# A second attention whose output is made one iteration earlier, with its norms on the scalar engine

## What is computed

```python
x = x + attention_a(layernorm(x))      # 16 heads of 8, rotary positions, causal, then a projection
x = x + experts(layernorm(x))
x = x + attention_b(layernorm(x))
x = x + experts(layernorm(x))          # the same expert weights

def attention_b(h):                    # one head of 128
    q, k, v = h @ WQ, h @ WK, h @ WV
    score = (q @ k.T / sqrt(128)) * band    # outside of the band (32 back, 31 ahead) the score is 0, not masked
    return softmax(score) @ v

def experts(h):                        # 64 experts of 128x128 and 128x128, the best 4 of each row
    s = sigmoid(h @ expert_sel.T)
    gates = s at its four largest, else 0
    return sum over experts e of (relu(h @ keys[e]) * gates[:, e]) @ values[e]
```

## Time and profile before

| | |
|---|---|
| time, median of 3 runs | 1121.22 us (1119.34 to 1125.25) |
| time of the profiled execution | 1114.41 us |
| its span, first to last instruction | 1112.7 us |
| PE busy, mean granted clock | 800.1 us (72%), 0.854 |
| DVE busy | 741.7 us (67%) |
| POOL busy | 727.1 us (65%) |
| ACT busy | 566.7 us (51%) |
| 16 DMA engines | 147 GB/s on average |

### The profile page before, as it was taken

How to read it: one execution, slowest core, us unless ns; L and a number is a source line. 1 busy time by engine, 2 the same in 40 slices (tenths; PEclk the granted TensorE clock), 3 DMA queues, 4 the chain that set the end, 5 groups by cost and what they waited for, 6 DMA issues and landing times.

```text
span 1112.7 us, 22610 instructions
## 1 busy us (share of the span) xinstructions
PE 800.1 (72%) x7290; PEld 584.2 (53%) x7290; DVE 741.7 (67%) x2033; ACT 566.7 (51%) x1513; POOL 727.1 (65%) x860
## 2 busy tenths in 40 slices
PE   1789988788878877679779766655556899898000
PEld 0444443444434432579779765444445888898000
DVE  3687898888878842576465666888979575576111
ACT  1167767675757665456536444444344556465000
POOL 6245748887875758665666462477777656666776
PEclk8689999998989988889979888776667999899555
DMA  6456645543237223359868651011113778898322
GB/s 192 135 197 209 211 164 197 175 137 100 84 94 236 61 70 101 107 161 270 237 172 245 174 141 37 29 50 52 50 52 103 216 215 240 233 270 250 93 61 64
DMA packets 206547, 163.82 MB, mean 147 GB/s; under 512 B 15968, under 2 KB 191072, under 8 KB 206432
## 3 DMA queue, kind: packets, MB, share of 16 engines
q1 hardware_dynamic: 183968, 110.43, 34.4%
q0 software_dynamic: 16384, 33.59, 10.2%
q10 hardware_dynamic: 6080, 18.35, 4.4%
HBM read 78.94 MB, written 83.36 MB: 146 GB/s over the span
## 4 chain that ended last, share of the span: by engine, by line
PE 36%; POOL 19%; DVE 17%; issue 12%; DMA 9%; ACT 6%; POOLq 0%; ACTq 0%; SPq 0%; DVEq 0%
PE ps L789 7%; PE ps L798 6%; POOL sorted_rows L1736 5%; PE ps L690 5%; DMA x_scaled<-result_rows,dest 3%; PE ps L778 3%; PE ps L649 3%; POOL y_heads L1750 2%; ACT arena L1001 2%; POOL arena L1782 2%; DVE row_max L1236 2%; POOL x_scaled L1750 2%; POOL xn L1757 2%; PE ps L698 1%; DVE block_max L1236 1%
## 5 line engine op out<-in xcount | busy, mean ns | idle before, releaser
L1001 ACT ACTIVATE arena<-ps 128x512 f32<-128x512 f32 x320 | 183.0, 598 | 74.5 <-PE ps L622 73.2
L1736 POOL DMA_INDIRECT sorted_rows<-v_aug,dest x128 | 128.4, 1003 | 86.6 <-DVE dest L1423 36.1
L1736 POOL DMA_INDIRECT sorted_rows<-x_scaled,dest x128 | 126.4, 987 | 43.1 <-issue 28.0
L789 PE MATMUL ps<-arena 128*128 128x128 f32 x1024 | 144.9, 287 | 10.3 <-DVE arena L1435 8.9
L1435 DVE COPY arena<-ps 128x512 f32<-128x512 f32 x128 | 88.3, 690 | 94.2 <-PE ps L778 93.7
L649 PE MATMUL ps<-arena 64*128 64x128 bf16 (+3 forms) x576 | 129.0, 302 | 28.5 <-DMA arena<-k_parts 15.1
L1236 DVE TENSOR_REDUCE row_max<-ps 128x1 f32<-128x512 f32 (+1 forms) x192 | 126.9, 681 | 30.7 <-PE ps L669 29.5
L990 ACT COPY arena<-ps 128x512 f32<-128x512 f32 x128 | 74.9, 585 | 137.1 <-PE ps L798 136.9
L798 PE MATMUL ps<-arena 128*128 x1024 | 139.4, 281 | 0.9 <-ACT arena L990 0.9
L789 PEld LDWEIGHTS ps<-arena 128*128 128x128 f32 x1024 | 132.7, 202 | 13.3 <-DVE arena L1435 9.9
L622 PE MATMUL ps<-arena 64*128 64x512 bf16 (+3 forms) x512 | 124.4, 311 | 16.2 <-ACT arena L1001 13.5
(11 more groups left out here) (221 smaller groups left out, 1648.8 us busy)
## 6 DMA issues: line engine op xcount, KB each, us to landing
arena<-sorted_rows SPq DMA_DIRECT2D x128, 256.0 KB
result_rows<-arena SPq DMA_DIRECT2D x128, 256.0 KB
sorted_rows<-arena ACTq DMA_DIRECT2D x16, 1024.0 KB, 5.0
arena<-q_parts SPq DMA_DIRECT2D x16, 512.0 KB, 4.0
arena<-k_parts SPq DMA_DIRECT2D x16, 512.0 KB, 5.0
q_parts<-parts SPq DMA_DIRECT2D x52, 128.0 KB, 2.9
k_parts<-parts SPq DMA_DIRECT2D x38, 128.0 KB, 3.0
sorted_rows<-x_scaled,dest POOLq DMA_INDIRECT x128
```

Source lines behind the costliest of these rows:

```text
L789: mm = pe.matmul(ps[:, e_bank(2, layer, half, n), P * i:P * i + P], ktile[:, v, P * i:P * i + P], xtt[:, v, P * i:P * i + P], start=True, ...
L1001: nc.scalar.activation(prob[:, grp % 2, pr % 2, PROB_AT[u]:PROB_AT[u] + T], ps[:, v % 2, :], ACT.Exp, scale=SCALE_A).then_inc(exp_done, 1)
L1736: g.indirect_dma_start(sorted_d[b // HALF][:, :], bass.IndirectOffsetOnAxis(dest[:, 16 * b + n:16 * b + n + 1], 0), scaled_rows(layer, b)[ ...
```

## The change

1. O of batch b+1 is made in iteration b, no longer O of b. For that PE's list now begins with S01, S23, then RK and VO, and P01, P23, O follow ahead of NT. The banks are dealt out anew.
2. The norms N3 and N2 leave DVE. DVE makes one more small product (minus mean times inverse root), and ACT applies them as `Identity` with a scale and a bias for each row, behind place 6 and ahead of its copy of NT.
3. On ACT the 16 scaled copies now both stand ahead of E, with the copy of VO ahead of them, and E stands directly ahead of the copy of P01.
4. The outside sums move on DVE from behind the norms to behind place 0; the first part of the positions moves from behind place 5 to ahead of it.
5. The rounding in `positions` is one operation, and the running sum starts from the page ends of the batch before, which saves another; the outside sums are one reduction over overlapping windows of five strips, which saves two. Positions are also computed in the first attention, so two operations go there as well.
6. The steps beside: (0, 1) had 16, 14 and 4 in iterations -2, -1 and 0, and now has 14, 11, 5 and, in iteration 1, 4. (1, 0) had 8 and 14 in iterations 7 and 8 and now has 9 and 14.

```diff
-BJOBS = [(7, "P01", 0), (1, "P23", 0), (5, "O", 0), (1, "S01", 1), (3, "S23", 1), (1, "RK", -1), (5, "NT", 0), (6, "LG", 0),
-         (3, "XT", 2), (6, "Q", 2), (7, "K", 2), (3, "V", 2), (5, "VO", 1), (6, "TB", -1)]
+BJOBS = [(1, "S01", 1), (3, "S23", 1), (6, "RK", -1), (7, "VO", 1), (7, "P01", 1), (1, "P23", 1), (5, "O", 1), (3, "NT", 0),
+         (1, "LG", 0), (7, "XT", 2), (3, "Q", 2), (7, "K", 2), (1, "V", 2), (6, "TB", -1)]
-BESIDE = {(0, 1): {-2: (3,) + 13 * (1,), -1: PLACES * (1,), 0: (1, 0, 0, 1, 0, 0, 1, 0, 0, 1, 0, 0, 0, 0)},
-          (1, 0): {7: 6 * (0,) + 8 * (1,), 8: PLACES * (1,)}}
+BESIDE = {(0, 1): {-2: (2,) + 12 * (1,) + (0,), -1: (0, 1, 1, 0) + 9 * (1,) + (0,), 0: (0, 1, 0, 1, 0, 1, 0, 1, 0, 1, 0, 0, 0, 0),
+                   1: (0, 1, 0, 1, 0, 1, 0, 1, 0, 0, 0, 0, 0, 0)},
+          (1, 0): {7: 5 * (0,) + 9 * (1,), 8: PLACES * (1,)}}
...
             for it in range(FIRST_IT_B, LAST_IT_B + 1):
+                attend(it, "S01", "S23")
+                beside(it, 0)
+                attend(it, "RK", "VO")
+                beside(it, 1)
+                beside(it, 2)
                 attend(it, "P01")
-                beside(it, 0)
+                beside(it, 3)
                 attend(it, "P23")
-                beside(it, 1)
+                beside(it, 4)
                 attend(it, "O")
-                beside(it, 2)
-                attend(it, "S01", "S23")
-                beside(it, 3)
-                attend(it, "RK")
-                beside(it, 4)
                 beside(it, 5)
+                beside(it, 6)
                 attend(it, "NT")
-                beside(it, 6)
+                beside(it, 7)
                 attend(it, "LG")
...
+            def apply_norm(i, b, dst, done):
+
+                for t in range(TT):
+                    nc.scalar.activation(dst[:, t, :], x[:, TT * b + t, :], ACT.Identity, bias=negb[:, i, t:t + 1],
+                                         scale=rsb[:, i, t:t + 1]).then_inc(done, 1)
...
+                if name == "N3":
+                    act.wait_ge(shifts, b + 3)
+                    act.wait_ge(scaled, 16 * (B + b - 1))
+                    apply_norm(1, b, xn1[:, b % 2], norm3)
+                    return
+                if name == "N2":
+                    act.wait_ge(shifts, b + 1)
+                    apply_norm(0, b, xn0, norm2)
+                    return
...
                 if 0 <= r < B:
                     act.wait_ge(top_seq, 12 * (B + r) + 12)
                     act.wait_ge(norm3, TT * r + TT)
                     scale(1, r, range(0, 8))
-                beside(it, 2)
-                beside(it, 3)
-                attend(it, "E")
+                beside(it, 1)
                 if 0 <= r < B:
                     scale(1, r, range(8, 16))
-                beside(it, 4)
-                beside(it, 5)
-                attend(it, "NT")
-                beside(it, 6)
+                beside(it, 2)
+                attend(it, "E", "P01")
+                beside(it, 3)
+                attend(it, "P23")
+                for place in (4, 5, 6):
+                    beside(it, place)
+                attend(it, "N3", "N2", "NT")
+                beside(it, 7)
...
+                nc.vector.scalar_tensor_tensor(out=negb[:, lo:hi, :], in0=mvb[:, lo:hi, :, 0], scalar=-1.0, in1=rs,
+                                               op0=ALU.mult, op1=ALU.mult).then_inc(shifts, 1)
...
-                nc.vector.tensor_scalar(near_pages[:, :], part_pages[:, :], MAGIC, None, ALU.add).then_inc(pos_seq, 1)
+                nc.vector.tensor_scalar(pages[:, q, :], part_pages[:, :], MAGIC, -MAGIC, ALU.add, ALU.add).then_inc(pos_seq, 1)
...
-                nc.vector.tensor_tensor_scan(upto[:, :], ones_f[:, :], fresh[:, :], 0.0, ALU.mult, ALU.add).then_inc(pos_seq, 1)
...
-                nc.vector.tensor_scalar(ends[:, h, :], upto[:, :], taken, None, ALU.add).then_inc(pos_seq, 1)
+                nc.vector.tensor_tensor_scan(ends[:, h, :], ones_f[:, :], fresh[:, :], taken, ALU.mult, ALU.add).then_inc(pos_seq, 1)
...
-                nc.vector.tensor_tensor(pairs[:, :], strips[:, 0:15], strips[:, 1:16], ALU.add).then_inc(strip_seq, 1)
-                dve.wait_ge(strip_seq, q + 3)
-                nc.vector.tensor_tensor(four[:, :], pairs[:, 4:11:2], pairs[:, 6:13:2], ALU.add).then_inc(strip_seq, 1)
-                dve.wait_ge(strip_seq, q + 4)
...
-                nc.vector.tensor_tensor(outside[:, :], four[:, :], strips[:, 3:10:2], ALU.add).then_inc(strip_seq, 1)
+                tail = strips[:, 3:14]
+                windows = bass.AP(tail.tensor, tail.offset, [tail.ap[0], (2, TT), (1, 5)])
+                nc.vector.tensor_reduce(outside[:, :], windows, AX.X, ALU.add).then_inc(strip_seq, 1)
...
                 beside(b, 0)
+                if 0 <= b + 1 < B:
+                    outside_sums(b + 1)
                 beside(b, 1)
...
-                if attend:
-                    dve.wait_ge(scaled, 16 * (B + b - 1))
-                    apply_norm(1, b, xn1[:, b % 2], norm3)
-                if prepare:
-                    if far:
-                        bank, n = bjob["XT", far - 1]
-                        dve.wait_ge(bank_ready[bank], n + 1)
-                    apply_norm(0, far, xn0, norm2)
                 beside(b, 4)
-                if 0 <= b + 1 < B:
-                    outside_sums(b + 1)
-                beside(b, 5)
                 if route:
                     bank, n = bjob["RK", r]
                     place_rows = positions(B + r, ps[:, bank, :], bank_ready[bank], n + 1, bank_free[bank], n + 1)
                     advance(place_rows, 6)
+                beside(b, 5)
                 beside(b, 6)
```

58 lines of the change are left out of this document (21 added, 37 removed).

## The result

| | before | after |
|---|---|---|
| time, median of 20 runs each | 1118.28 us (1112.73 to 1127.92) | 1124.33 us (1120.40 to 1130.33) |
| ratio, 95% interval | | 1.005 (1.0032 to 1.0068) |
| profiled execution, its span | 1114.41, 1112.7 us | 1123.67, 1121.9 us |
| PE busy, granted clock | 800.1 us, 0.854 | 812.7 us, 0.855 |
| DVE busy | 741.7 us | 718.8 us |

The changed kernel is 0.5% slower, 5.6 us by the ratio (0.005 of 1118.28; the two medians themselves differ by 6.05). DVE has 23 us less to do, as meant, and the end comes later all the same. The two profiled executions lie 9.3 us apart, more than the runs do. Of that, 2.0 us are there before the changed part begins: the first expert step of half (0, 1) (DVE's copy) is at 559.62 instead of 557.65.

What follows compares the result with a forecast made beforehand. No engine fills the span; POOL's run sets the end, by when destinations of batches 0 and 7 and expert results come. +1.4 and -0.9 gave +0.5 us: 1114.9 profiled, 1121.5 with the 6.8 carried over; range 1110 to 1129.

Steps and rivals of the forecast that it cites:

- rival B: ACT's order: in iteration 5 E, P and N3 wait behind scaled copies whose end POOL decides; slower, 1128 us; 20%.
- first scatter: Start of POOL's run, when batch 0's destinations are ready: 700.6 us, so -5.5, bounds -10 and +1.
- the hold: In iteration 5 ACT's scaled copies of batch 4 wait for POOL's scatter of batch 2, last issued at 810.36 us.
- the ninth step: Iteration 7 has 9 expert steps instead of 8 on the way to batch 7's destinations: +2.2 us.
- Scaled copies of batch 4: Their end on ACT in iteration 5, moved with the first scatter: 812.9 - 5.5 = 807.4 us.
- From there to the choice of batch 5: From the last scaled copy through E, P, O (1.95), NT and LG: 10 us, where it was 4.9.
- The ring: The late round of PE and ACT: 27.7 us at half clock, 24 with some products at full clock, 25.7 taken.
- Choice of batch 6 to the first step of (1, 0): It was 11.9 us; 1.1 of norms less and 0.2 more, so the first step comes at 854.1.
- destinations 7: The moment batch 7's destinations are ready for POOL's scatter: -0.3 + 2.2 - 0.5 = +1.4 us.
- Norm on ACT: Priced like the scaled copy, 0.30 us each, N3 1.2 us on the path to NT; wrong if over 0.4.
- Waits: O's wait gone, PE idle ahead of P01 not NT, S01 waiting 1.1 us for V's copies, scatter 7 about 10.
- Rival A: The early output wins through with PE at full clock, the end following POOL alone: -8.5 to -11.5, about 1111; 27%.

Runs made afterwards that it cites:

- before_swap: The kernel before with other buffers for the scaled rows of batches 4, 5 and 7, so batch 4's copies aren't held by batch 2's scatter; ratio 0.9921.
- Norms_on_dve: The changed kernel with the norms N3 and N2 back on DVE, all else kept; ratio 1.0046.
- before_short: The kernel before with only the shorter positions and outside sums (four DVE operations fewer a batch); ratio 0.9979.
- swap_late_table: swap_homes, and in addition DVE takes the page table of half 0 behind the choice of the next iteration; ratio 0.9911.
- swap_homes: The changed kernel with other buffers for the scaled rows of batches 4, 5 and 7, so ACT doesn't wait for batch 2's scatter; ratio 0.998.
- best1: swap_late_table, and in addition the scaled copies of batches 1 to 5 stand behind V's copies on ACT; ratio 0.991.
- before_swap_short: The kernel before with the buffer exchange of before_swap and the shorter positions and outside sums of before_short; ratio 0.9956.
- best1_old: best1 with the tables of expert steps of the kernel before; ratio 0.9948.

## Why the prediction was right in its number and wrong in its mechanism

I forecast 1121.5 us, and it was 1124.33, inside 1110 to 1129. But that stood on a base of 1121.22 for the kernel before, whose runs beside the changed one have a median of 1118.28. As a difference I said +0.3 us (my sum reads +0.5, and carried over with its 6.8 it gives 1121.7, not 1121.5) and it is +5.6, at the border of what I called no change. What happened is rival B, which I gave 20%: E, P and N3 behind held copies, in the place and nearly at the price that I named (1128 is 6.8 above the base). That the number held is in part luck: B was in the range, not in the forecast. The size is a near match too, since B assumed no gain at the first scatter, where there were 3.1 us, and a cheaper O. And B holds for this pair of kernels: before_swap shows that the hold costs the kernel before as much, and without it the change still stands behind by as much (0.998 against 0.9921), until the page table is taken later. So it is shown where the loss arises in this kernel, and that it goes with the hold; how it divides between the longer chain behind the hold, the longer round and the ninth step is read from single traces alone.

Along the steps, with moments on the clock of the prediction, so 2.0 us of later start taken off:

- *First scatter, 700.6 said.* 704.91 - 1.97 = 702.9. The gain is 3.1 us, not 5.5, inside the bounds of -10 and +1. Norms_on_dve (149.5) shows that it comes from the norms, and before_short that the shorter operations bring none of it (148.6).
- *Scaled copies of batch 4, 807.4 said.* 813.53 - 1.97 = 811.6. Besides the 2.3 from above, POOL's run to there took 1.7 us longer than before. I had taken its pace as fixed, though the rows of its timeline aren't all alike (1.0 and 1.1 us here, and up to 1.9 in places), and the 144 transfers up to scatter 7 take 1.38 us each (199.4 / 144), not the 1.25 to 1.3 that I read.
- *From there to the choice of batch 5, 10.0 said.* It is 11.6 (825.10 - 813.53). **The term that was mis-sized is O: 1.95 said, 3.54 measured.** I took it from the kernel before, where PE goes from Q, K, V through VO and P to O with no idle over 0.91 us. The new order leaves only S, RK, VO and an idle of 6.5 us ahead of P01; I had that idle in the sum and yet kept O at the full clock. Every late round has it.
- *The ring, 24 to 27.7, 25.7 taken.* Measured 28.4 in the last round (853.47 - 825.10), 0.7 above the far end, which had O at 1.9 and not 3.54; the other terms came to 0.9 less. "Nearer the middle" was the choice that failed: the idle of "some 7 us" that I named as the ground for the half clock was there, so the half-clock end was the value to take, for O too.
- *Choice of batch 6 to the first step of (1, 0), 11.0 said:* 11.05. Right.
- *From there to destinations 7, 52.8 said (51.1 + 2.2 - 0.5).* 50.3 (914.83 - 864.52). The ninth step was priced at 2.2 and costs 3.3 in the traces; something else in this stretch is 3.6 us shorter, and I haven't taken it apart. Before_short shows 0.8 of it: 61.7 us from choice 6 to scatter 7 against 63.0, where the sum had 0.5.
- *Norm on ACT, 0.30 us each said.* A single one is 481 ns, and eight take 3.19 us, a pitch of 0.39. The prediction called itself wrong above 0.4 and didn't say of which: the duration is above it, the pitch just below. It costs nothing at the end, since O at the half clock covers it.
- *Waits.* O's wait is gone, PE idles ahead of P01 and not of NT, V's copies hold S01 for 1.15 us: as said. The wait ahead of scatter 7 is 15.42, not about 10. The wait for the page table (9.55 us at 794.39) I hadn't foreseen. TB is last in PE's list, and DVE takes it last in its own iteration; with DVE ahead of PE, it waits there for PE's whole ring. The hold covers it in this kernel; without the hold swap_late_table is 7.7 us below swap_homes by the ratios (0.998 - 0.9911) and 5.0 at the end of the trace.
- *Rival A* (the early output wins through) is what best1 shows for the ring: 22.9 us once the copies are out of E's way. Its price, though, was bounded by POOL, as I said of A ("the end then follows POOL alone").

The largest error of the reasoning is that the 4.9 and 10 us behind the hold were both in my walk, one in each kernel, and I let an early first scatter pay for it. The first scatter was worth 3.1 us, and POOL's run took more than half of it back before it reached the hold.

## What to carry to other kernels

Before work is moved behind a waiting instruction, follow that engine's list and ask which of the instructions ahead is held by another engine's run: the chain behind the hold counts in full, however much idle the engine has elsewhere. When the matrix engine gets only short groups of products between idles, price them by rows at the half clock, all of them. The idle directly ahead doesn't tell it alone: O is at the full clock behind 5.93 us of idle with an expert step in between, and at the half one in best1 behind 2.25 us. And when one engine (here POOL) issues without a break to the end, look for the gain in when it starts and in what keeps buffers from it, since a shorter ring elsewhere (27.8 to 22.9 us from swap_late_table to best1, both at 0.991) doesn't show in the time. Ask also which waits a hold covers: they come free when it goes.

## What the runs showed of the hardware

- A second per-row operand of an ACTIVATE of 128x128 costs 92 ns: 389 ns with a scale, 481 with scale and bias, and the pitch of eight in a row goes from 0.29 to 0.39 us ((2.45 - 0.39) / 7 and (3.19 - 0.48) / 7). The Trainium skill (ScalarE: Activation LUTs, What ACT_TABLE_LOAD costs) says about 93 ns for each pointer operand; the trace agrees.
- The same product of O takes 275 ns (median of 64) before and 421 after, with the granted clock at 0.75 and 0.63 in the stretches of 813 to 854 and 813 to 866 us. The idle directly ahead isn't the whole of it. In iterations 0 and 1 of the kernel after PE idles 5.93 and 5.57 us ahead of P01, whose four transposes take 1.09 us; an expert step stands between, and the next four take 0.60 and O's first pair 0.46. In best1 PE idles 2.25 us, P01's four transposes take 0.63, and O's first pair 0.77, at a granted clock of 0.60 from 820.79 to 827.60 us. Over the whole run PE is busy 12.6 us more (812.7 against 800.1).
- POOL's pace isn't fixed: the same 144 transfers took 143.5, 146.7, 144.3 and 144.3 us of busy time in before_swap, before_swap_short, best1 and best1_old, and 192.1, 196.7, 198.9 and 199.6 us with the gaps between them, none of it a wait for destinations. Single ones take from 0.94 to 2.0 us. These differences are of the size of the effects sought here. The gaps are longer where the scatters wait more for earlier ones to land (waits of over 0.45 us: 4.4 us in before_swap, 6.3 in before_swap_short, 10.3 and 11.1 in the other two); why single transfers are longer stays open.
